# Expert weight preparation moved wholly into the attention steps, POOL's half of it tied to the accumulator's finish, in an MoE and attention block

## The chip, the cores and the metric

One core of one Trainium2 chip. The metric is the device time of one launch in microseconds (us), shown for the kernel before as the median of three runs. Engines are named as in the profile: PE (TensorE), DVE (VectorE), ACT (ScalarE), POOL (GpSimd), SP (SyncE, which here only issues DMAs).

## What is computed

Input q holds 8 x 512 tokens of 256 values. The output is q plus an attention of the normalized tokens against 1024 shared keys and values, plus a mixture of experts (one shared expert, eight routed ones, two chosen per token):

```python
xn = _layernorm(x)                                  # 4096 tokens x 256
scale = xn[:, ::step].reshape(b, -1)                # one factor per key, from 4 rows of each batch
qk = einsum('bsd,btd->bst', xn, k) * scale[:, None, :]
attn = einsum('bst,btv->bsv', softmax(qk), v)
shared = gelu(xn @ Wfc_s + bfc_s) @ Wproj_s + bproj_s
for e in range(8):                                  # gate: softmax over the two best experts
    h = gelu(xn @ Wfc[e] + bfc[e]) @ Wproj[e] + bproj[e]
    routed = routed + h * gate[:, e:e + 1]
return x + attn + (shared + routed)
```

All inputs are float32. The kernel multiplies in float16 with each operand split into a high half and a low residual, three products for each (high x high, high x low, low x high).

## The kernel before, in words

The kernel is one hand-ordered program. Each engine has its own list of instructions, written out in the order in which it runs, and the engines meet only at semaphores. Four stretches follow one another on PE:

- **Front steps** (i = 1 to 7, after a start-up for tile 0). Tokens come in 16 tiles of 256. A step computes the shared expert of tile i (`up_shared`, L1266; `down`, L1286), routes the tile (router L1238, `rank` L1249 to L1252), and transposes the next tile (`tr1`, L1202), which DVE copies to `x_t` (`copy_xt`, L794). DVE also makes the layer norm (`front_a`, `normalize` L844), the float16 split of it (`split_x_hi` L853, `split_x_lo` L858) and the slot numbers (`front_b`, its first instruction L874).
- **Attention steps** (u = 0 to 31, one for 128 queries). PE's list for a step is `transpose_probs(u)` L1352, `scores(u + 2)` L1338, `side_work(u)`, `values(u - 1)` L1406. `side_work` carries the routing of tiles 8 to 15: by u modulo 3, the router, the rank (L1249), or the transposition of a further tile. DVE's list is `finish(u - 2)` L991 (which adds the attention output to the accumulator `acc`), `p_lo(u)` L979 and L982, then in a step with u mod 3 = 0 the normalization L844, in the next one the split L853 and L858, then `scale_scores(u + 2)` L968, then the routing work (L808 to L836, or L874 to L888). ACT runs `p_hi(u)` L744, a piece of weight preparation, `exp(u + 2)` L735.
- **Routed steps**: 40 steps for blocks of tokens sorted by expert, in which SP loads the expert's packed weights from `wpack` (`load_fc`, `load_pj`, L462), the tokens (`load_slots`, L499) and the biases. The first block's tokens are transposed by PE already in attention step 29 (`tr2_first`, L1202), from the tile that SP loads first.
- **Last steps**: the shared expert for tiles 8 to 15, and POOL's gathers of routed results (L666), which DVE adds to `acc`.

The weight preparation is 16 jobs, one for each of the 8 experts' two matrices (1 MB each). SP loads a matrix to `w_stage` (`load_job`, L365), ACT scales it in place (`scale_w`, L676) and casts its high half to `w_split` (`split_w_hi`, L684), POOL subtracts (`split_w_lo`, L609: two halves of four 256-wide instructions each), and SP stores the 1 MB result to `wpack` (`store_job`, L375). Before, there are two buffers of each kind; four jobs run in the front steps (i = 1, 3, 5, 7) and twelve in attention steps 0 to 24. POOL also computes the reciprocal deviation of each tile (`inv_std`, L592), scatters the split tokens to `slots_x` (L619, four indirect DMAs for a tile), and adds the shared expert's output bias to each tile of `acc` (`add_bias`, L600), for which DVE's `evict_shared` and `finish` wait. The function names with their lines are all in the printed code:

```python
            for u in range(QT):
                k, phase = u // 3, u % 3
                i = NA + 1 + k
```

sets the phases named here; NA is 8, QT is 32, tile i is normalized, split and transposed in phases 0, 1 and 2.

## Time and profile before

| what | value |
|---|---|
| median of 3 runs | 867.32 us (866.02 to 872.22) |
| the profiled execution, its own time | 861.36 us |
| its span in the profile | 859.5 us |
| PE busy | 785.8 us, 91% of the span |
| DVE, ACT, POOL busy | 490.7, 441.0, 257.3 us |
| instructions | 20915 |

The span runs from the first to the last recorded instruction. 1.86 us of the execution's own time lie outside it. Windows are given in us from the span's start. The attention steps' matmuls run from 117.8 to 354.7 us of it, the routed steps from there to about 742 us. In the timelines a row is one instruction or a run of like ones; its first two numbers are start and duration, "x24" is the count, and the bracket at its end the idle time before it and what ended it.

### The profile page before, as it was taken

To read this page: it belongs to the slowest core of one execution; us is meant where nothing else is said; L and a number is where in the kernel's file an instruction comes from. 1 tells how busy PE (TensorE), PEld (TensorE's weight loads), DVE (VectorE), ACT (ScalarE), POOL (GpSimd) and SP (SyncE) were. 2 spreads that over 40 slices of the span, in tenths; PEclk is the share of its full clock that TensorE was granted. 3 is DMA by queue.
4 is the path that set the end of the run, shared out by engine and by line. 5 is a ranking of instruction groups with operands and counts; after the bars stand their busy time and mean duration, and the time that the engine had idled before them with its cause. 6 is when DMAs were issued, how large, how long until landed. Compare 5 with 4: busy or idle time off the path is not lost.

```text
span 859.5 us, 20915 instructions
## 1 busy us (share of the span) xinstructions
PE 785.8 (91%) x7222; PEld 661.5 (77%) x7222; DVE 490.7 (57%) x1144; ACT 441.0 (51%) x845; POOL 257.3 (30%) x318
## 2 busy tenths in 40 slices
PE   4888899699969899999999999999999999977893
PEld 3777776476647677999999989999999998865772
DVE  6888868888898776444434453333333333353464
ACT  6665466365636544565465555555555555524350
POOL 5666756557655730000000000000000000263655
PEclk9999999899979999999999999999999999996997
DMA  9464341647464535344322554454545452142334
GB/s 307 157 221 135 137 168 54 233 154 233 142 221 153 197 118 185 124 165 153 123 68 97 158 183 161 158 160 146 172 135 175 128 186 86 45 125 74 119 119 134
DMA packets 70379, 129.11 MB, mean 150 GB/s; under 512 B 12248, under 2 KB 56480, under 8 KB 63920
## 3 DMA queue, kind: packets, MB, share of 16 engines
q1 hardware_dynamic: 64176, 111.57, 39.3%
q0 software_dynamic: 6144, 16.79, 6.1%
q8 instruction: 33, 0.54, 0.2%
q14 instruction: 26, 0.21, 0.1%
HBM read 88.29 MB, written 40.04 MB: 149 GB/s over the span
## 4 chain that ended last, share of the span: by engine, by line
PE 69%; DVE 15%; issue 6%; POOL 4%; ACT 2%; DMA 2%; another core or an unknown queue 2%; DVEq 0%; SPq 0%; POOLq 0%; ACTq 0%
PE ps_h L1266 28%; PE ps_v L1286 27%; PE ps_v L1406 6%; PE ps_h L1338 4%; DVE xn L844 3%; PE ps_t L1202 2%; DVE prob L968 2%; POOL w_split L609 2%; PE ps_t L1352 1%; DVE p_t L982 1%; POOL y_rows L666 1%; DVE acc L1171 1%; DVE h_split L893 1%; ACT h L693 1%
## 5 line engine op out<-in xcount | busy, mean ns | idle before, releaser
L893 DVE TENSOR_TENSOR h_split<-h,h_split 128x512 f16<-128x512 f32 (+1 forms) x224 | 144.8, 655 | 164.0 <-ACT h_split L699 160.9
L693 ACT ACTIVATE h<-ps_h,b_fc 128x256 f32<-128x256 f32 (+1 forms) x320 | 125.9, 444 | 170.9 <-PE ps_h L1266 170.9
L666 POOL DMA_INDIRECT y_rows<-slots_y,y_row_all x64 | 64.4, 1007 | 480.9 <-DMA slots_y<-prob 437.8
L1266 PE MATMUL ps_h<-x_t,w_split 128*128 128x256 f16 (+1 forms) x1920 | 193.3, 261 | 0.0
L1286 PE MATMUL ps_v<-w_stage,h_split 128*128 128x256 f16 x1704 | 192.6, 273 | 0.0
L1266 PEld LDWEIGHTS ps_h<-x_t,w_split 128*128 128x128 f16 x1920 | 170.5, 98 | 17.0
L1286 PEld LDWEIGHTS ps_v<-w_stage,h_split 128*128 128x128 f16 x1704 | 165.1, 98 | 18.4
L699 ACT CAST h_split<-h 128x512 f16<-128x512 f32 (+1 forms) x224 | 131.1, 585 | 10.4 <-ACT h L693 0.4
L1266 PE MATMUL ps_h<-x_t,w_shared 128*128 128x256 f16 x768 | 94.0, 278 | 13.4 <-issue 13.0
L693 ACT ACTIVATE h<-ps_h,b_t 128x256 f32<-128x256 f32 x128 | 53.5, 468 | 99.6 <-PE ps_h L1266 58.1
L1266 PEld LDWEIGHTS ps_h<-x_t,w_shared 128*128 128x128 f16 x768 | 75.0, 99 | 29.4 <-issue 19.8
L1286 PE MATMUL ps_v<-w_shared,h_split 128*128 128x256 f16 x768 | 93.0, 280 | 3.5 <-issue 3.2
L1406 PE MATMUL ps_v<-v_split,p_t 128*128 128x256 f16 x768 | 93.0, 280 | 0.0
L1286 PEld LDWEIGHTS ps_v<-w_shared,h_split 128*128 128x128 f16 x768 | 76.6, 100 | 15.3 <-issue 4.5
L1338 PE MATMUL ps_h<-k_t,x_t 128*128 128x512 f16 x384 | 88.1, 379 | 0.0
L609 POOL TENSOR_TENSOR w_split<-w_stage,w_split 128x256 f16<-128x256 f32 x128 | 85.3, 699 | 4.0 <-ACT w_split L684 4.0
L619 POOL DMA_INDIRECT slots_x<-x_split,pos_i x64 | 65.0, 1016 | 69.4 <-DVE pos_i L888 53.2
L1406 PEld LDWEIGHTS ps_v<-v_split,p_t 128*128 128x128 f16 x768 | 75.5, 100 | 11.4
L1115 DVE SCALAR_TENSOR_TENSOR prob<-ps_v,b_pj 128x256 f32<-128x256 f32 x71 | 30.2, 425 | 87.0 <-PE ps_v L1286 87.0
L735 ACT ACTIVATE prob<-prob,neg_max 128x1024 f32<-128x1024 f32 x32 | 36.8, 1149 | 81.6 <-DVE neg_max L972 78.5
L1338 PEld LDWEIGHTS ps_h<-k_t,x_t 128*128 128x128 f16 x384 | 37.6, 98 | 38.1
L968 DVE CUSTOM_DVE_ANT_0 prob<-ps_h,scale_b 128x1024 f32<-128x1024 f32 x32 | 39.0, 1219 | 15.1 <-PE ps_h L1338 12.1
(153 smaller groups left out, 624.4 us busy)
## 6 DMA issues: line engine op xcount, KB each, us to landing
w_split<-wpack SPq DMA_DIRECT2D x17, 1024.0 KB, 5.1
w_stage<-wpack SPq DMA_DIRECT2D x17, 1024.0 KB, 5.0
wpack<-w_split SPq DMA_DIRECT2D x16, 1024.0 KB, 5.1
w_stage<-in_L_ffn_Wfc_dram SPq DMA_DIRECT2D x8, 1024.0 KB
w_stage<-in_L_ffn_Wproj_dram SPq DMA_DIRECT2D x8, 1024.0 KB
x_split<-slots_x SPq DMA_DIRECT2D x31, 256.0 KB, 3.5
slots_y<-prob SPq DMA_DIRECT2D x31, 256.0 KB, 3.2
b_pj<-in_L_ffn_bproj_dram SPq DMA_DIRECT2D x40, 128.0 KB, 3.1
```

Of the source, the lines that this page charges most:

```text
L609: ins = g.tensor_tensor(dst[:, 2048 + at:2304 + at], w_stage[par][:, at:at + 256], dst[:, at:at + 256], ALU.subtract)
L619: g.indirect_dma_start(slots_x, bass.IndirectOffsetOnAxis(ap=pos_i[par][:, c:c + 1], axis=0), x_split[i % 3][:, a, :], None).then_inc(s_sc ...
L666: g.indirect_dma_start(y_rows[:, n, kk, :], None, slots_y, bass.IndirectOffsetOnAxis(ap=y_row_all[:, c:c + 1], axis=0)).then_inc(s_gat[n], 16)
L693: ins = nc.scalar.activation(h32[:, hc, 0:n], ps_h[:, hc * TILE:hc * TILE + n], ACT.Gelu_apprx_tanh, bias=bias[:, hc:hc + 1], scale=1.0 / WS)
L699: nc.scalar.copy(h_split[par][:, 0, 2 * b:2 * b + 2, 0:n], h32[:, 2 * b:2 * b + 2, 0:n]).then_inc(s_hhi, 1)
L735: nc.scalar.activation(prob[par][:, :], prob[par][:, :], ACT.Exp, bias=neg_max[par][:, 0:1], accum_out=row_sum[par][:, 0:1]).then_inc(s_ex ...
L893: ve.tensor_tensor(h_split[par][:, 1, 2 * b:2 * b + 2, 0:n], h32[:, 2 * b:2 * b + 2, 0:n], h_split[par][:, 0, 2 * b:2 * b + 2, 0:n], ALU.s ...
L968: ve.tensor_tensor_reduce(out=prob[par][:, :], in0=ps_h[:, par * KEYS:(par + 1) * KEYS], in1=scale_b[b % 2][:, :], scale=1.0, scalar=-3.0e ...
L1266: ins = mm(ps_h[:, hc * TILE:hc * TILE + cols], wv[:, wl, c, hc * P:(hc + 1) * P], x[:, xl * DC + c, 0:cols], start=n == 0, stop=n == 3 * ...
L1286: ins = mm(ps_y[a][:, :], h_split[par][:, xl, c, a * P:(a + 1) * P], wv[:, wl, c, :], start=n == 0, stop=n == 3 * HC - 1)
L1338: ins = mm(ps_h[:, lo:lo + 512], x_t[:, i, ql * DC + c, par * P:(par + 1) * P], k_t[:, kl * DC + c, half * 512:(half + 1) * 512], start=n ...
L1406: ins = mm(ps_y[par][:, :], p_t[par][:, pl, c, :], v_split[:, vl, c, :], start=n == 0, stop=n == 3 * KC - 1)
```

## The change

The 16 jobs all run in the attention steps. There are four buffers for the loaded weights and four for the split ones: the two old pairs, and beside them `y_rows` and `h32` (loads), and the two `h_split` buffers (results), which the attention steps leave unused. Jobs 0 to 9 take two steps each (ACT scales at u = 2n and casts at 2n + 1, POOL subtracts one half in each of the two steps after that); jobs 10 to 15 have both of ACT's instructions in one step (u = 20, 21, 22, 24, 25, 26) and both of POOL's halves in one, two steps later (the last in step 28). A half is one 1024-wide instruction, no longer four of 256, and POOL waits before it for `finish(u - 2)`, DVE's first instruction of the step. In DVE's list `scale_scores` comes before the normalization and the split. `inv_std` runs at the start of the step in which the tile is normalized, no longer at the end of the one before. All 16 bias adds come after the last attention step, and only the last steps wait for them. The store of the last job is issued by SP after step 28, before it waits for all stores and loads the first routed weights.

```diff
+        stages = [t[:, :] for t in w_stage] + [y_rows[:, :, :, :].rearrange("p g k d -> p (g k d)"),
+                                               h32[:, :, :].rearrange("p c n -> p (c n)")]
+        splits = [t[:, :] for t in w_split] + [t[:, :, :, :].rearrange("p h c n -> p (h c n)") for t in h_split]
...
-        JOB_B = 2 + NA // 2
-        JOBS = 2 + 2 * EXPERTS
+        JOBS = 2 * EXPERTS
+        SLOW = 10
+
+        def scale_slot(n):
+
+            return 2 * n if n < SLOW else 2 * SLOW + (n - SLOW) + (n - SLOW) // 3
+
+        def hi_slot(n):
+            return 2 * n + 1 if n < SLOW else scale_slot(n)
+
+        def lo_slot(n, half):
+            return 2 * n + 2 + half if n < SLOW else scale_slot(n) + 2
...
-                if u % 2 == 0:
-                    m = JOB_B + u // 2
-                    if m <= JOBS:
-                        store_job(m - 1)
-                    if m + 1 < JOBS:
-                        load_job(m + 1)
+                if u == 0:
+                    load_job(3)
+                for n in range(JOBS):
+                    if u == lo_slot(n, 1) + 1:
+                        store_job(n)
+                        if n + 4 < JOBS:
+                            load_job(n + 4)
...
-                for at in range(piece * 1024, piece * 1024 + 1024, 256):
-                    ins = g.tensor_tensor(dst[:, 2048 + at:2304 + at], w_stage[par][:, at:at + 256], dst[:, at:at + 256],
-                                          ALU.subtract)
-                ins.then_inc(s_wlo, 1)
+                at = piece * 1024
+                g.tensor_tensor(dst[:, 2048 + at:3072 + at], src[:, at:at + 1024], dst[:, at:at + 1024],
+                                ALU.subtract).then_inc(s_wlo, 1)
...
-                add_bias(i)
-                if job_of(i) is not None:
-                    split_w_lo(job_of(i), 0)
-                    split_w_lo(job_of(i), 1)
...
+                if phase == 0 and i < SHARED:
+                    inv_std(i)
+                if u == 0:
+                    scatter(NA - 1)
+                for n in range(JOBS):
+                    for half in range(2):
+                        if u == lo_slot(n, half):
+
+                            wait_ge(pool, s_fin, u - 1)
+                            split_w_lo(n + 2, half)
+                if phase == 2 and i - 1 < SHARED:
+                    scatter(i - 1)
+
+
+            wait_ge(pool, s_bpj_in, 16)
+            wait_ge(pool, s_fin, QT)
+            for i in range(SHARED):
+                add_bias(i)
...
                 if u == 30:
                     act.wait_ge(s_bfc_in[0], 16)
+                    act.wait_ge(s_wlo, 2 * (JOBS + 1))
+                    act.wait_ge(s_w_out[2], 16 * (JOBS // 4))
                     gelu(R0, 0, b_fc[0], banks=(0, 1))
...
             def finish(u):
                 par = u % 2
-                dve.wait_ge(s_bias, u // SUB + 1)
...
                 p_lo(u)
+                if u + 2 < QT:
+                    scale_scores(u + 2)
                 if phase == 0 and i < SHARED:
                     front_b(norm=i)
                 if phase == 1 and i < SHARED:
                     front_b(split=i)
-                if u + 2 < QT:
-                    scale_scores(u + 2)
```

POOL's order in the first attention steps, before (L592 is the reciprocal deviation, L609 the halves of a job, L600 the bias add, L619 the scatter):

```order
L619 DMA slots_x<-x_split,pos_i 34048x512 x4
L592 TENSOR_TENSOR rstd<-var_eps,neg_half 128x2
L609 TENSOR_TENSOR w_split<-w_stage,w_split 128x256 x8
L600 TENSOR_TENSOR acc<-acc,b_pj_s 128x512
L609 TENSOR_TENSOR w_split<-w_stage,w_split 128x256 x8
L619 DMA slots_x<-x_split,pos_i 34048x512 x4
```

and the same place in the change (L602, L616 and L625 are those instructions):

```order
L602 TENSOR_TENSOR rstd<-var_eps,neg_half 128x2
L625 DMA slots_x<-x_split,pos_i 34048x512 x4
L616 TENSOR_TENSOR w_split<-w_stage,w_split 128x1024
L625 DMA slots_x<-x_split,pos_i 34048x512 x4
L602 TENSOR_TENSOR rstd<-var_eps,neg_half 128x2
L616 TENSOR_TENSOR w_split<-w_stage,w_split 128x1024 x3
L625 DMA slots_x<-x_split,pos_i 34048x512 x4
```

Where 17 of POOL's instructions (8 pieces, a bias add, 8 more pieces) stood in a row, single halves stand now, each behind a wait for DVE's finish.

DVE's order in attention step 0 of the next tile (L979 and L982 are `p_lo`, L844 the normalization, L968 and L972 `scale_scores`), before:

```order
L979 RECIPROCAL inv_sum<-row_sum 128x1
L982 TENSOR_TENSOR p_t<-ps_t,p_t 128x512 x2
L844 TENSOR_SCALAR xn<-acc,mean_var,rstd 128x256 x2
L968 ISA prob,row_max<-ps_h,scale_b 128x1024
L968 ISA row_max 128x1
L972 TENSOR_SCALAR neg_max<-row_max 128x1
```

and in the change:

```order
L988 RECIPROCAL inv_sum<-row_sum 128x1
L991 TENSOR_TENSOR p_t<-ps_t,p_t 128x512 x2
L977 ISA prob,row_max<-ps_h,scale_b 128x1024
L977 ISA row_max 128x1
L981 TENSOR_SCALAR neg_max<-row_max 128x1
L854 TENSOR_SCALAR xn<-acc,mean_var,rstd 128x256 x2
```

The normalization has moved behind the scaling of the scores.

## Rows read from the trace of the kernel before

**Rows 1.** Windows: length, busy us (x count) of PE, PEld, DVE, ACT, POOL, then clock, DMA.

```profile
38.00:117.80 79.80, 71.71 (x732) 63.33 (x729) 68.29 (x205) 48.52 (x82) 55.28 (x59) 0.98 0.46 156
117.80:354.70 236.90, 217.01 (x1679) 157.98 (x1678) 183.48 (x472) 124.18 (x167) 116.05 (x155) 0.96 0.48 163
354.70:742.00 387.30, 387.30 (x3894) 351.21 (x3892) 157.09 (x280) 206.03 (x480) 0.00 (x0) 1.00 0.44 143
```

**Rows 2.** Timeline of PE, attention steps 4, 27, 28 and 29.

```profile
162.73 0.19 PE L1249 MATMUL ps_v<-mask,before 128*128 128x8 f16 x1 [7.68 <-DVE acc L991]
...
162.89 4.59 PE L1406 MATMUL ps_v<-v_split,p_t 128*128 128x256 f16 x24
...
320.94 1.04 PE L1352 MATMUL ps_t<-ident_f,prob 128*128 128x128 f32 x8
...
327.02 1.04 PE L1352 MATMUL ps_t<-ident_f,prob 128*128 128x128 f32 x8
...
336.57 0.61 PE L1202 MATMUL ps_v<-ident_h,x_split 128*128 128x128 f16 x8
337.02 2.78 PE L1406 MATMUL ps_v<-v_split,p_t 128*128 128x256 f16 x24
```

**Rows 3.** Timeline of DVE, attention steps 3, 6, 27 and 28.

```profile
149.50 9.56 DVE L844 TENSOR_SCALAR xn<-acc,mean_var,rstd 128x256 f32<-128x256 f32 x2
...
176.60 1.16 DVE L844 TENSOR_SCALAR xn<-acc,mean_var,rstd 128x256 f32<-128x256 f32 x2
...
328.27 0.16 DVE L1014 TENSOR_SCALAR tab_x<-step_r 1x22 int32<-1x22 f32 x1 [0.19 <-issue]
328.41 0.48 DVE L991 SCALAR_TENSOR_TENSOR acc<-ps_v,inv_sum,acc 128x256 f32<-128x256 f32 x1
```

**Rows 4.** Timeline of POOL, start-up and attention steps 3 and 6.

```profile
10.49 2.12 POOL L625 TENSOR_TENSOR w_shared<-w_stage,w_shared 128x1024 f16<-128x1024 f32 x1 [4.48 <-ACT w_shared L710]
...
147.28 5.07 POOL L609 TENSOR_TENSOR w_split<-w_stage,w_split 128x256 f16<-128x256 f32 x8
...
153.54 5.05 POOL L609 TENSOR_TENSOR w_split<-w_stage,w_split 128x256 f16<-128x256 f32 x8
...
175.64 5.18 POOL L609 TENSOR_TENSOR w_split<-w_stage,w_split 128x256 f16<-128x256 f32 x8
```

**Rows 5.** Groups of DVE by shape, 117.8 to 354.7 us (busy, mean ns, idle before).

```profile
L982 DVE TENSOR_TENSOR p_t<-ps_t,p_t 128x512 f16<-128x512 f32 x64 | 40.9, 681 | 3.5 <-ACT p_t L744 3.5
L968 DVE CUSTOM_DVE_ANT_0 prob<-ps_h,scale_b 128x1024 f32<-128x1024 f32 x32 | 39.0, 1219 | 15.1 <-PE ps_h L1338 12.1 <-issue 2.9
L844 DVE TENSOR_SCALAR xn<-acc,mean_var,rstd 128x256 f32<-128x256 f32 x14 | 24.8, 1812 | 0.0
```

**Rows 6.** Groups of DVE by shape, 38 to 117.8 us.

```profile
L874 DVE TENSOR_TENSOR mask_sum<-mask_sum,mask 128x8 f16<-128x8 f16 x6 | 6.6, 1105 | 0.3 <-PE ps_t L1252 0.3
```

**Rows 7.** Waits, 38 to 117.8 us: total, times, longest.

```profile
PE ps_t L1202 <- DVE k_t L939: 4.1, 2, 2.2
PE ps_t L1238 <- DVE x_t L794: 4.0, 4, 1.7
```

**Rows 8.** Groups of ACT by shape, 117.8 to 354.7 us.

```profile
L735 ACT ACTIVATE prob<-prob,neg_max 128x1024 f32<-128x1024 f32 x32 | 36.8, 1149 | 81.6 <-DVE neg_max L972 78.5 <-issue 3.1
L744 ACT CAST p_t<-ps_t 128x512 f16<-128x512 f32 x64 | 34.2, 584 | 13.0 <-PE ps_t L1352 12.7
L676 ACT ACTIVATE w_stage<-w_stage 128x2048 f32<-128x2048 f32 x12 | 23.0, 1918 | 12.9 <-DMA w_stage<-in_L_ffn_Wproj_dram 12.9
```

**Rows 9.** Timeline of SP's queue, first loads for the routed steps.

```profile
329.26 0.37 SPq L462 DMA_DIRECT2D w_split<-wpack  x1
...
331.12 1.50 SPq L499 DMA_DIRECT2D x_split<-slots_x  x2
```

**Rows 10.** DMA issues: size of one, median us to landing.

```profile
wpack<-w_split SPq DMA_DIRECT2D x16, 1024.0 KB, 5.1
...
x_split<-slots_x SPq DMA_DIRECT2D x31, 256.0 KB, 3.5
```

More of the change, by code:

```diff
@@ L223, in moe_attention_block @@
         s_row_out = sem2("s_row_out")
-        s_w_in = sem2("s_w_in")
-        s_w_out = sem2("s_w_out")
+        s_wproj_in = sem("s_wproj_in")
+        s_w_in = [sem(f"s_w_in{n}") for n in range(4)]
+        s_w_out = [sem(f"s_w_out{n}") for n in range(4)]
         s_bt_out = sem("s_bt_out")
@@ L329, in rows @@
             return ap[ds(first, n), :].rearrange("(a p) d -> p a d", p=P)
-        def stored(m):
-            return 16 * ((m - 2) // 2)
-        def job_of(i):
-            return 2 + i // 2 if i % 2 == 1 and i < NA else None
-        JOB_B = 2 + NA // 2
-        JOBS = 2 + 2 * EXPERTS
+        JOBS = 2 * EXPERTS
[6 more added lines that the diff above has]
+            return 2 * n + 2 + half if n < SLOW else scale_slot(n) + 2
         block = ctx.enter_context(nc.Block())
@@ L374, in store_job @@
                     dst = wpack[(n - EXPERTS) * P:(n - EXPERTS + 1) * P, 4096:8192]
-                sp.dma_start(dst, w_split[m % 2][:, :]).then_inc(s_w_out[m % 2], 16)
+                sp.dma_start(dst, splits[n % 4]).then_inc(s_w_out[n % 4], 16)
             def store_row(i):
@@ L509, in store_slots @@
                 sp.dma_start(dst, src).then_inc(s_y_out[par], 16)
-            for par in range(2):
-                wait_ge(sp, s_w_out[par], 16 * EXPERTS)
+            for n in range(4):
+                wait_ge(sp, s_w_out[n], 16 * (JOBS // 4))
             wait_ge(sp, s_bt_out, 16)
@@ L673, in scale_w @@
             def scale_w(m):
-                par = m % 2
-                act.wait_ge(s_w_in[par], 16 * ((m + par) // 2))
-                nc.scalar.mul(w_stage[par][:, :], w_stage[par][:, :], WS).then_inc(s_wsc, 1)
+                src = w_stage[1][:, :] if m == 1 else stages[(m - 2) % 4]
+                if m == 1:
+                    act.wait_ge(s_wproj_in, 16)
+                else:
+                    act.wait_ge(s_w_in[(m - 2) % 4], 16 * ((m - 2) // 4 + 1))
+                nc.scalar.mul(src, src, WS).then_inc(s_wsc, 1)
             def split_w_hi(m):
-                par = m % 2
-                dst = w_shared[1] if m == 1 else w_split[par]
+                n = m - 2
+                src = w_stage[1][:, :] if m == 1 else stages[n % 4]
+                dst = w_shared[1][:, :] if m == 1 else splits[n % 4]
                 act.wait_ge(s_wsc, m)
-                if m >= 4:
-                    act.wait_ge(s_w_out[par], stored(m))
-                nc.scalar.copy(dst[:, 0:2048], w_stage[par][:, :]).then_inc(s_whi, 1)
+                if n in (2, 3):
+                    act.wait_ge(s_mm2, 2 * NA)
+                if n >= 4:
+                    act.wait_ge(s_w_out[n % 4], 16 * (n // 4))
+                nc.scalar.copy(dst[:, 0:2048], src).then_inc(s_whi, 1)
             def gelu(t, par, bias, first=False, n=TILE, banks=range(BANKS)):
@@ L716, in _ @@
                 gelu(i, i % 2, b_s)
-                if job_of(i) is not None:
-                    scale_w(job_of(i))
-                    split_w_hi(job_of(i))
                 if i == 2:
@@ L756, in _ @@
                     act.wait_ge(s_bfc_in[0], 16)
+                    act.wait_ge(s_wlo, 2 * (JOBS + 1))
+                    act.wait_ge(s_w_out[2], 16 * (JOBS // 4))
                     gelu(R0, 0, b_fc[0], banks=(0, 1))
-                m = JOB_B + u // 2
-                if m < JOBS:
-                    if u % 2 == 0:
-                        scale_w(m)
-                    else:
-                        split_w_hi(m)
+                for n in range(JOBS):
+                    if u == scale_slot(n):
+                        scale_w(n + 2)
+                    if u == hi_slot(n):
+                        split_w_hi(n + 2)
                 if u + 2 < QT:
```

57 lines of the change are left out of this document (23 added, 34 removed).

## The prediction

> **What bounds the kernel now.** I read the windows first. From 354.7 us PE is busy in every microsecond of the routed stretch, 387.30 of 387.30, and POOL does nothing there [rows 1]. Nothing in that stretch can get shorter by moving POOL's or ACT's work. What can change lies before it: the front steps leave PE idle for 79.80 - 71.71 = 8.1 us, the attention steps for 236.90 - 217.01 = 19.9 us [rows 1]. Then I asked the timelines what those 19.9 us are. They are not spread out. At attention step 4 PE stands for 7.68 us before its rank matmul and is released by DVE's finish, and the values matmuls behind it take 4.59 us, where the same 24 take 2.78 later [rows 2]. So a stall costs PE its length and 1.8 us more at a lower clock. The granted clock of the whole stretch, 0.96 against 1.00 in the routed steps, says the same [rows 1].
>
> DVE's timeline shows where it was: in step 3 the two normalizations took 9.56 us; in step 6 the same two took 1.16 [rows 3]. POOL ran 8 subtractions from 147.28 and 8 more from 153.54 to 158.59, and the normalization ended at 159.06 [rows 3, 4]. DVE did not compute for 9 us, it was shut out while POOL worked. Over the attention steps 14 normalizations have 24.8 us of busy time, a mean of 1812 ns [rows 5]. Two that are left alone take at most 1.16 us together [rows 3], which would make 8.1 us for 14, so at least 16.7 us went in this one line. Its neighbours, which read scores and probabilities from PSUM, are not touched: `p_lo` has a mean of 681 ns over 64 and the scaling 1219 ns over 32 [rows 5]. That difference is what the change rests on.
>
> The Trainium skill, "SBUF — State Buffer", section "Who interferes with whom", gives the mechanism: a VectorE copy, cast or tensor_scalar between SBUF operands can take the port pair that it shares with GpSimd, and whichever engine starts first keeps the pair until its instruction ends. The trace agrees on who is blocked, and not on how long: by that rule DVE would get in after one 256-wide piece, 5.07 / 8 = 0.63 us, while here it waited over all 17 pieces [rows 3, 4]. In step 6 it did get in early, 1.16 us beside a burst that ran from 175.64 to 180.82 [rows 3, 4]. By the rule taken strictly a 1024-wide piece blocks longer than a 256-wide one did (2.12 us against 0.63); that speaks against this part of the change and is rival 2.
>
> **The change, part by part.** The sum is made against the profiled execution.
>
> *Attention stalls.* POOL's half now starts when DVE has ended its first instruction of the step. A 1024-wide subtraction took 2.12 us at start-up, and four 256-wide ones in the attention steps 5.07 / 2 = 2.54 us [rows 4]. I take 2.12, the row of the same shape, and keep 2.54 as the other end. In that time DVE runs `p_lo` (2 x 0.68) and then the scaling (1.22): 2.58 us that read PSUM and are not blocked [rows 5], and in a step that PE bounds it waits for scores besides. The normalization comes behind both, so POOL has left by then in either case. In a step after a scatter POOL is late by some 2 us, but so is the normalization, behind PE's scores. What goes is PE's 19.9 us of idle time [rows 1] and two low-clock stretches of 1.8 us [rows 2]; I take all 23.5 us, and for the range 12 of it at the lower end. What is late next is PE itself: 6.08 us from one step to the next in steps 27 to 28 [rows 2].
>
> *Front steps.* POOL loses 8 pieces in each of four steps and a bias add in all seven, ACT 3.8 us in four steps. DVE's first routing instruction of a step, an addition of 128x8, has a mean of 1105 ns [rows 6]; 8 values in each partition are no work for 1105 ns where the scaling needs 1219 ns for 1024, so I read most of 6 x 1.1 = 6.6 us as blocked time; and the addition stands ahead of the x_t copy for which PE waits 4.0 us [rows 7]. This wait goes. PE's other wait, 4.1 us for the copied keys in two steps [rows 7], I let go by half, since in those steps DVE also carries the splits of keys and values. 8.1 - 2.1 = 6.0 us, and 1 us more for the same effect in the start-up step: 7 us, between 4 and 9.
>
> *ACT.* In the last six jobs both passes, 1.92 us each if the cast is as long as the scaling, come into one step beside an exponential and two casts: 3.84 + 1.15 + 1.17 = 6.2 us [rows 8] against PE's 6.08 [rows 2]. Three such steps in a row put ACT some 0.5 us behind. The exponential has waited 78.5 us for DVE in these 32 steps [rows 8], and it is made two steps ahead of its use. No cost; up to 3 us if semaphores add 0.5 a step.
>
> *The bias adds.* All 16 go to the routed steps, where POOL is idle for 387 us [rows 1], and are first wanted at 742 us. No cost. Behind them in POOL's list are only the gathers. The waits of DVE for them are gone.
>
> *The end of the attention steps.* This is where the change adds a wait. Before, the last job was stored at about step 24, and SP's wait for all stores was long over when DVE's tables were ready at 328.43; then the first weight load was issued at 329.26 and the token loads at 331.12 [rows 3, 9]. Now the last job's two halves wait for the finish of step 28, which ended at 328.89 [rows 3]. On that clock: 328.89 + 2 x 2.12 [rows 4] = 333.1; the store takes 5.1 us to land [rows 10] = 338.3 with 0.1 us for the issue; from there SP needs to the token load what it needed before, 331.12 - 328.43 = 2.69 us [rows 3, 9], and the tokens 3.5 us to land [rows 10] = 344.5. PE reached the transposition of these tokens at 336.57 and values(28) stands right behind it in PE's list [rows 2]. So PE stands still for 344.5 - 336.57 = 8 us in step 29, and if it ends like the other stalls it costs 1.8 us of low clock: 9.8 us. Bounds: 6 if the store lands quickly, 13 if POOL is a few us behind from the scatter of step 23 or needs 2.54 us a half. Two of the weights' loads come behind this too, but their users come later than the tokens' by more.
>
> *Sum.* 859.5 - 23.5 - 7 + 9.8 = 838.8 us of span; with the 1.9 us outside it 840.7. The median of the runs shown is 6.0 us above the profiled execution. If the length of DVE's shut-out is a matter of chance, as 9.56 against 1.16 suggests, part of those 6 us is that chance and goes too. I keep half: 843.7, forecast 844 us.
>
> **The rivals.**
>
> 1. *No stall in step 29* (POOL or the store is earlier than I think, or PE comes later). For it: in the 6.2 us steps of ACT, PE could slip by a little. Against it: the finish that opens the last half is at a fixed place of DVE's list. 844 - 9.8 = 834 us.
>
> 2. *The blocking only moves.* POOL comes out of the scatter late (four indirect DMAs in a step that also has a half), and the half behind it meets the normalization. One whole piece, 2.12 us [rows 4], is lost in each meeting. Seven tiles are normalized in these steps: 7 x 2.12 = 14.8 us, 859 us. Against it: the last seven normalization steps would all have to meet it, though DVE has 2.58 us of unblocked work first. The rule of the Trainium skill quoted above is this rival's, one instruction and no more.
>
> 3. *The long shut-outs are not POOL's bursts at all*, or come back in another line, and only the front's gain and the new stall are real: 844 + 23.5 = 867 us, no change. Against it is the match of the times, 158.59 and 159.06.
>
> 4. *Slower: the gate makes every half a collision.* If one of the instructions right behind the finish is in fact blocked by a 1024-wide POOL instruction, the gate aligns the two engines in every step. 20 steps carry one half, at 2.12 us each: 42 us, 886 us. It decides from the point where DVE's first blockable instruction comes within 2.12 us of the finish. Against it: the means of 681 and 1219 ns hold over steps both with and without POOL's work [rows 5]; they would have to hold only for short pieces.
>
> **How the numbers follow.** Forecast 0.55 (its own range 834 to 853), rival 1 0.13, rival 2 0.14, rival 3 0.11, rival 4 0.07. The range for 8 in 10 is 830 to 864: down to rival 1 with a few us more from the front, up past rival 2 but short of rival 3. A measurement of this kernel can tell about 1%, that is 858.6 and 876.0 us. Faster by over 1%: the forecast, rival 1 and half of rival 2, 0.75. Within 1%: the other half and rival 3, 0.18. Slower: rival 4, 0.07.
>
> **What would show it.** In the changed profile the normalizations' mean should be near 0.4 to 0.6 us and none above 2.5; PE's waits for DVE's finish in the rank should be under 2 us in all; the front stretch should be some 7 us shorter; the first routing addition should fall from 1.1 us to a few tenths; and the transposition of the first tokens in step 29 should stand for about 8 us, released by a DMA, with slow values matmuls behind it. If PE is idle in the middle of the attention steps by more than 5 us, the main step is wrong; if it isn't idle in step 29, the last one is.

## The result, and the profile after

The change makes the kernel faster: 845.55 us median (836.54 to 846.22, four runs) against 866.67 us (862.83 to 872.22, four runs of the kernel before). The ratio is 0.9728, with a 95% interval of 0.9656 to 0.98. The profiled execution took 836.54 us, its span is 834.7 us. The forecast of 844 us is met; what follows shows that two of its terms missed and, by luck, nearly cancelled.

I cut the span at the first scores matmul, at the first routed matmul behind the last attention step (two halves of the first block's up matmuls already run inside steps 30 and 31) and at the first matmul of the last steps. The change moved 10.3 us in the front, 13.9 in the attention steps and nothing after them:

| stretch | before | after |
|---|---|---|
| start-up and front steps | 117.8 us | 107.5 us |
| attention steps | 236.9 us | 223.0 us |
| routed steps | 377.3 us | 377.6 us |
| last steps | 127.5 us | 126.6 us |

The windows of the kernel after, with the columns of [rows 1]:

```profile
38.00:107.50 69.50, 66.90 (x703) 59.90 (x701) 55.65 (x188) 36.89 (x74) 28.47 (x29) 1.00 0.33 106
107.50:330.40 222.90, 214.12 (x1679) 157.57 (x1677) 158.10 (x471) 139.02 (x174) 108.06 (x75) 0.98 0.56 194
330.40:717.50 387.10, 387.02 (x3889) 350.68 (x3888) 166.06 (x280) 205.69 (x480) 23.78 (x16) 1.00 0.44 143
```

PE's idle time in the front steps fell from 8.1 us [rows 1] to 2.6, in the attention steps from 19.9 us [rows 1] to 8.8. POOL's 16 bias adds, 23.78 us, now lie under a PE that is busy for 387.02 of 387.10 us. DVE's busy time in the attention steps fell from 183.48 us [rows 1] to 158.10, though it does the same work there. The groups of DVE by shape in that stretch say which line lost most of these 25.4 us (busy, mean ns, idle before):

```profile
L991 DVE TENSOR_TENSOR p_t<-ps_t,p_t 128x512 f16<-128x512 f32 x64 | 41.5, 681 | 6.5 <-issue 3.6 <-ACT p_t L752 2.5
L977 DVE CUSTOM_DVE_ANT_0 prob<-ps_h,scale_b 128x1024 f32<-128x1024 f32 x32 | 39.2, 1224 | 20.2 <-PE ps_h L1347 20.2
L854 DVE TENSOR_SCALAR xn<-acc,mean_var,rstd 128x256 f32<-128x256 f32 x14 | 5.3, 420 | 0.0
L863 DVE CAST x_split<-xn 128x512 f16<-128x512 f32 x7 | 3.0, 426 | 0.5 <-issue 0.4
```

The 14 normalizations take 5.3 us where they took 24.8 [rows 5], 19.5 us less. The lines that read PSUM have kept their durations to within 5 ns, with POOL's 1024-wide halves beside them. The scaling, which waited 12.1 us for PE's scores [rows 5], waits 20.2: DVE is now ahead of PE. The small routing addition of the front steps has lost its blocked time too, 152 ns against 1105 [rows 6] (groups of DVE by shape, 20 to 107.46 us):

```profile
L884 DVE TENSOR_TENSOR mask_sum<-mask_sum,mask 128x8 f16<-128x8 f16 x8 | 1.2, 152 | 0.0
```

One step shows how the two engines pass each other. First DVE's timeline, then POOL's:

```profile
128.55 0.43 DVE L863 CAST x_split<-xn 128x512 f16<-128x512 f32 x1
...
130.82 0.49 DVE L999 SCALAR_TENSOR_TENSOR acc<-ps_v,inv_sum,acc 128x256 f32<-128x256 f32 x1
131.41 0.16 DVE L988 RECIPROCAL inv_sum<-row_sum 128x1 f32<-128x1 f32 x1
131.49 1.27 DVE L991 TENSOR_TENSOR p_t<-ps_t,p_t 128x512 f16<-128x512 f32 x2
132.70 1.23 DVE L977 CUSTOM_DVE_ANT_0 prob<-ps_h,scale_b 128x1024 f32<-128x1024 f32 x1
```

```profile
131.51 2.14 POOL L616 TENSOR_TENSOR w_split<-w_stage,w_split 128x1024 f16<-128x1024 f32 x1 [5.83 <-DVE acc L999]
133.80 0.99 POOL L625 DMA_INDIRECT slots_x<-x_split,pos_i  x1
```

POOL waited 5.83 us for the finish, worked from 131.51 to 133.65 while DVE read PSUM until 133.93, and was gone. In a step with a normalization the margin is thinner, since POOL's scatter and the reciprocal deviation stand ahead of the half. DVE, then POOL, in the next such step:

```profile
141.13 0.79 DVE L854 TENSOR_SCALAR xn<-acc,mean_var,rstd 128x256 f32<-128x256 f32 x2
```

```profile
139.31 2.12 POOL L616 TENSOR_TENSOR w_split<-w_stage,w_split 128x1024 f16<-128x1024 f32 x1
```

The half ends at 141.43, 0.3 us after the normalization has begun, and costs it less than 0.1 us (0.79 us for the pair against 0.73 in the quickest). The new wait stands where the forecast put it. PE's timeline in attention steps 28 to 30:

```profile
299.46 2.75 PE L1347 MATMUL ps_h<-k_t,x_t 128*128 128x512 f16 x12
310.16 1.03 PE L1211 MATMUL ps_v<-ident_h,x_split 128*128 128x128 f16 x8 [7.95 <-DMA x_split<-slots_x]
310.98 4.57 PE L1415 MATMUL ps_v<-v_split,p_t 128*128 128x256 f16 x24
```

PE stands for 7.95 us, and the values matmuls behind it take 4.57 us, where undisturbed ones take 2.78 [rows 2]. POOL's timeline and SP's queue show the chain that leads there:

```profile
294.73 4.22 POOL L616 TENSOR_TENSOR h_split<-h,h_split 128x1024 f16<-128x1024 f32 x2 [2.51 <-DVE acc L999]
```

```profile
292.29 7.08 SPq L384 DMA_DIRECT2D wpack<-h_split  x2
304.26 0.37 SPq L472 DMA_DIRECT2D w_split<-wpack  x1
...
306.11 1.51 SPq L509 DMA_DIRECT2D x_split<-slots_x  x2
```

The last two halves end at 298.95; some 5 us later, the time that such a store takes to land [rows 10], SP goes on to the routed loads (304.26) and the tokens (306.11), which PE gets at 310.16.

### The profile page after: what moved, and what is told of

The parts are those of the page before. It is cut to its first block, busy times and chain, and to the rows that moved or that the text cites. A ratio compares the mean times of both kernels' runs of the same rounds, so it can differ in the third digit from the quotient of the medians.

```text
span 834.7 us, 20811 instructions
## 1 busy us (share of the span) xinstructions
PE 780.4 (93%) x7222; PEld 659.7 (79%) x7222; DVE 462.7 (55%) x1144; ACT 441.4 (53%) x845; POOL 240.8 (29%) x216
## 4 chain that ended last, share of the span: by engine, by line
PE 82%; DVE 8%; issue 4%; another core or an unknown queue 2%; DMA 2%; POOL 2%; SPq 1%; ACT 0%; POOLq 0%; DVEq 0%
PE ps_h L1275 29%; PE ps_v L1295 28%; PE ps_v L1415 10%; PE ps_h L1347 9%; PE ps_t L1361 3%; PE ps_t L1211 2%; DVE h_split L903 2%; DVE acc L1179 1%; POOL y_rows L671 1%; DMA b_rows<-in_L_ffn_bfc_s_dram 1%; DVE xn L854 1%; DMA wpack<-h_split 1%; PE ps_v L1211 0%; DMA x_split<-slots_x 0%
## 5 line engine op out<-in xcount | busy, mean ns | idle before, releaser
L903 DVE TENSOR_TENSOR h_split<-h,h_split 128x512 f16<-128x512 f32 (+1 forms) x224 | 152.9, 692 | 160.4 <-ACT h_split L710 152.9
L710 ACT CAST h_split<-h 128x512 f16<-128x512 f32 (+1 forms) x224 | 130.8, 584 | 10.1
L1275 PE MATMUL ps_h<-x_t,w_shared 128*128 128x256 f16 x768 | 93.3, 278 | 14.3 <-issue 13.7
L1295 PE MATMUL ps_v<-w_shared,h_split 128*128 128x256 f16 x768 | 91.2, 275 | 9.1 <-issue 9.0
L1415 PE MATMUL ps_v<-v_split,p_t 128*128 128x256 f16 x768 | 90.8, 276 | 0.0
L625 POOL DMA_INDIRECT slots_x<-x_split,pos_i x64 | 64.1, 1002 | 17.5 <-issue 16.7
L977 DVE CUSTOM_DVE_ANT_0 prob<-ps_h,scale_b 128x1024 f32<-128x1024 f32 x32 | 39.2, 1224 | 20.2 <-PE ps_h L1347 20.2
L752 ACT CAST p_t<-ps_t 128x512 f16<-128x512 f32 x64 | 34.9, 585 | 26.0 <-PE ps_t L1361 25.5
```

What stands on the lines that cost most here:

```text
L625: g.indirect_dma_start(slots_x, bass.IndirectOffsetOnAxis(ap=pos_i[par][:, c:c + 1], axis=0), x_split[i % 3][:, a, :], None).then_inc(s_sc ...
L710: nc.scalar.copy(h_split[par][:, 0, 2 * b:2 * b + 2, 0:n], h32[:, 2 * b:2 * b + 2, 0:n]).then_inc(s_hhi, 1)
L752: nc.scalar.copy(p_t[par][:, 0, 4 * kk:4 * kk + 4, :], ps_t[:, kk * 512:(kk + 1) * 512].rearrange("p (c n) -> p c n", n=P)).then_inc(s_phi, 1)
L903: ve.tensor_tensor(h_split[par][:, 1, 2 * b:2 * b + 2, 0:n], h32[:, 2 * b:2 * b + 2, 0:n], h_split[par][:, 0, 2 * b:2 * b + 2, 0:n], ALU.s ...
L977: ve.tensor_tensor_reduce(out=prob[par][:, :], in0=ps_h[:, par * KEYS:(par + 1) * KEYS], in1=scale_b[b % 2][:, :], scale=1.0, scalar=-3.0e ...
L1275: ins = mm(ps_h[:, hc * TILE:hc * TILE + cols], wv[:, wl, c, hc * P:(hc + 1) * P], x[:, xl * DC + c, 0:cols], start=n == 0, stop=n == 3 * ...
```

## The experiments

By a shut-out I mean a DVE instruction that has begun and cannot proceed while POOL works; by the gate, POOL's wait for the finish ahead of each half. The theory: the time lay in DVE's shut-outs by runs of POOL instructions, and both the gate and the new order of DVE's list are needed to end them; what is left is the stall behind the last store. The rivals: the smaller number of instructions does it, or the order alone, or the gate alone, or the bias adds. The table has the stretches of each profiled execution (us), the median, and the ratio to the kernel before with its interval. Executions of the kernel before in these comparisons had medians of 864 to 869 us. A median of two runs can be off by several us, so I read the stretches first. They scatter too: four profiles with the front's code of the kernel before (the two in which only the order changed, the one with the gate alone, and its own) have fronts of 116.2 to 120.6 us, seven with the front's code of the change 106.9 to 108.9 us. Where the long shut-outs are gone and PE never stands at the end, the attention steps agree within 0.2 us (213.7, 213.7, 213.8).

| run | front | attention | last | median (runs) | ratio |
|---|---|---|---|---|---|
| 1024-wide pieces alone | 115.1 | 240.8 | 125.6 | 868.55 (6) | 0.9986 (0.9925 to 1.0047) |
| order alone | 120.6 | 233.4 | 128.8 | 863.35 (8) | 0.9987 (0.9953 to 1.0022) |
| bias adds alone | 114.7 | 225.8 | 134.8 | 856.71 (2) | 0.9859 (0.9758 to 0.996) |
| gate alone | 116.2 | 245.8 | 135.2 | 875.19 (2) | 1.0119 (1.002 to 1.0217) |
| change without gate | 107.1 | 228.2 | 133.3 | 848.22 (2) | 0.9761 (0.9676 to 0.9847) |
| change without order | 107.8 | 230.7 | 121.6 | 845.11 (2) | 0.972 (0.9628 to 0.9813) |
| change with 256-wide pieces | 107.7 | 224.7 | 132.7 | 839.66 (2) | 0.9658 (0.9578 to 0.9738) |
| jobs sooner | 108.9 | 213.7 | 134.5 | 834.02 (4) | 0.9588 (0.9565 to 0.961) |
| tokens first | 106.9 | 218.7 | 134.3 | 833.43 (2) | 0.9586 (0.9491 to 0.9681) |
| both of these | 107.3 | 213.7 | 135.1 | 833.27 (4) | 0.9621 (0.9543 to 0.9698) |
| jobs sooner, gathers cut | 107.7 | 213.8 | 96.4 | 797.89 (2) | 0.9225 (0.9136 to 0.9314) |

**1024-wide pieces alone**, on the kernel before.

```diff
-                for at in range(piece * 1024, piece * 1024 + 1024, 256):
-                    ins = g.tensor_tensor(dst[:, 2048 + at:2304 + at], w_stage[par][:, at:at + 256], dst[:, at:at + 256],
-                                          ALU.subtract)
-                ins.then_inc(s_wlo, 1)
+                at = piece * 1024
+                g.tensor_tensor(dst[:, 2048 + at:3072 + at], w_stage[par][:, at:at + 1024], dst[:, at:at + 1024],
+                                ALU.subtract).then_inc(s_wlo, 1)
```

> The kernel before with one edit: a half of a job is one 1024-wide POOL subtraction, not four of 256; nothing is gated and DVE's order is the old one. Theory A (DVE stays shut out as long as POOL's instructions follow one another without a pause): two halves, a bias add and two halves in a row still shut out the normalization for over 7 us in one or two places, its total in the attention steps stays at 15 to 25 us and PE stays idle there for 15 to 20 us. Theory B (the port is free at the end of each instruction, as the Trainium skill, SBUF, has it): no normalization takes longer than 2.2 + 0.4 us, its total falls below 15 us, PE's idle time there below 8 us. The time: A 858 to 870 us, B 845 to 855 us.

No change in the time (868.55 us, as theory A has it), and the clearest picture of the shut-out. PE idles 19.9 us in the attention steps, also as in A, but the normalizations take 34.5 us, more than the 15 to 25 expected, and the stretch is 3.9 us longer than before. DVE's timeline, then POOL's:

```profile
146.68 7.89 DVE L843 TENSOR_SCALAR xn<-acc,mean_var,rstd 128x256 f32<-128x256 f32 x2
154.50 1.21 DVE L967 CUSTOM_DVE_ANT_0 prob<-ps_h,scale_b 128x1024 f32<-128x1024 f32 x1
```

```profile
144.50 4.21 POOL L609 TENSOR_TENSOR w_split<-w_stage,w_split 128x1024 f16<-128x1024 f32 x2
148.68 1.26 POOL L600 TENSOR_TENSOR acc<-acc,b_pj_s 128x512 f32<-128x512 f32 x1
149.90 4.19 POOL L609 TENSOR_TENSOR w_split<-w_stage,w_split 128x1024 f16<-128x1024 f32 x2
```

POOL has five instructions in a row from 144.50 to 154.09. DVE's normalizations begin at 146.68 and end at 154.57: they sat behind four POOL instructions, past the boundaries at 148.7, 149.9 and 152.0, and got in when POOL stopped. The same happened at 193.40 (7.98 us) and at 238.70 (7.95 us), so three times, where one or two were expected. So a shut-out may last as long as POOL has instructions queued, whatever their width. This contradicts the Trainium skill, "SBUF — State Buffer", section "Who interferes with whom", by which the other engine gets the ports when the instruction that holds them ends; the measurement decides.

The other meetings here do go by that rule. Three more pairs here took 3.45, 3.07 and 3.38 us, each instruction of DVE getting in when one 1024-wide piece ended; beside 256-wide pieces the like pairs took 1.1 to 1.5 us. That is where the width counts, and why the total rose. A long queue does not decide it by itself either. At one step of the kernel before, the one that corresponds to 193.40 here, POOL had all 17 instructions in a row too, and each of DVE's two got in after one piece. DVE, then POOL:

```profile
196.19 1.51 DVE L844 TENSOR_SCALAR xn<-acc,mean_var,rstd 128x256 f32<-128x256 f32 x2
```

```profile
194.31 5.17 POOL L609 TENSOR_TENSOR w_split<-w_stage,w_split 128x256 f16<-128x256 f32 x8
199.44 1.28 POOL L600 TENSOR_TENSOR acc<-acc,b_pj_s 128x512 f32<-128x512 f32 x1
200.68 5.26 POOL L609 TENSOR_TENSOR w_split<-w_stage,w_split 128x256 f16<-128x256 f32 x8
```

What makes one meeting long and the other short no run tells.

**The order alone**, on the kernel before: `scale_scores(u + 2)` stands ahead of the normalization and the split. Two executions of it were profiled; the table has the second.

> The kernel before with DVE's order alone changed, once more for a profile of its own. As for b_swap: theory A, normalizations of over 5 us in one or two places, PE's idle time in the attention steps 12 to 20 us; rival, idle time under 6 us.

The ratio is 0.9987 over eight runs: POOL's 17 instructions outlast the 2.58 us that the order puts between them. One pair of normalizations still took 8.19 us, and PE idled 15.9 us, both as theory A has it. In the other profiled execution (872.25 us) two pairs were held off for so long (8.31 and 8.30 us), and the attention steps took 240.5 us. So the number of long shut-outs seems to differ between executions of one kernel.

**The bias adds alone**, on the kernel before: they move behind the attention loop, with DVE's waits for them.

```diff
-                if phase == 1 and i - 1 < SHARED:
-                    add_bias(i - 1)
...
+            wait_ge(pool, s_bpj_in, 16)
+            wait_ge(pool, s_fin, QT)
+            for i in range(SHARED):
+                add_bias(i)
```

> The kernel before with the bias adds alone moved behind the attention steps (and DVE's waits for them with them). Theory: the first routing addition in the front steps was blocked by the bias add behind the scatter: its mean there falls from 1105 ns to under 300, the front stretch up to the first scores gets 4 to 6 us shorter (117.8 to about 113), the rest of the 10 us that the changed kernel gained there is due to the jobs. Rival: the addition is blocked by the scatter's indirect DMAs or by the jobs: its mean stays above 700 ns and the front keeps within 1.5 us of 117.8. In the attention steps the bursts are one instruction shorter; the long shut-outs stay.

The front loses 3.1 us, a bit less than I expected, and DVE's first routing addition falls to 149 ns there, as in the full change. Of PE's two waits there, the one for the x_t copy fell from 4.0 us [rows 7] to 1.3, and the one for the keys stayed (6.0 us against 4.1); in the change they are 1.4 and 1.2. In the attention steps this execution had one long shut-out of the normalizations (8.51 us), the kernel before two (9.56 and 9.58), which one profile of each can't lay to the bias adds. So the bias adds are about a third of the front's 10.3 us, give or take the front's scatter. That the jobs which left it are the rest is a subtraction; no run moves them alone.

**The gate alone**, on the kernel before.

```diff
-                if u % 2 == 0 and JOB_B < JOB_B + u // 2 <= JOBS:
-                    split_w_lo(JOB_B + u // 2 - 1, 0)
-                    split_w_lo(JOB_B + u // 2 - 1, 1)
+                if JOB_B < JOB_B + u // 2 <= JOBS:
+                    wait_ge(pool, s_fin, u - 1)
+                    split_w_lo(JOB_B + u // 2 - 1, u % 2)
```

> The kernel before with the gate alone: in the attention steps each half of a job waits for the finish of its step, the second half in the next step; old job schedule (four in the front steps), two buffers, old DVE order, 256-wide pieces, bias adds in place. Theory A (the gate carries most of the attention steps' gain, the order the rest): no normalization over 4 us, but they stand close behind the finish and still meet a half, 10 to 20 us in all; and with two buffers ACT waits longer for the loads: the stretch falls from 236.9 to 222 to 230 us. Rival (the gate alone is enough): 214 to 218 us. Rival (two buffers are too few, ACT's wait for the weight load holds up exp): ACT waits over 25 us for DMA (12.9 before) and the stretch stays above 232 us.

Slower, by 1.2% (two runs, the interval 0.2 to 2.2%): theory A's stretch of 222 to 230 us missed, at 245.8, and the rival with too few buffers held. The normalizations did fall, to 11.5 us, though one still took 4.25, but a wait took their place. The waits from 100 to 370 us (total, times, longest):

```profile
ACT w_stage L676 <- DMA w_stage<-in_L_ffn_Wproj_dram: 43.2, 5, 11.3
...
PE ps_t L1352 <- DVE p_t L982: 17.3, 4, 5.8
ACT w_stage L676 <- DMA w_stage<-in_L_ffn_Wfc_dram: 15.0, 2, 12.0
```

ACT waits 58.2 us for weights, where it waited 12.9 [rows 8]. POOL gives a buffer back a step later, the load behind it starts later, ACT's probabilities stand in its list behind the late weights, and PE waits for them through DVE. With two buffers the gate costs more than it saves. In the change, with four, ACT does not wait for a weight load at all in the attention steps. The gate with four buffers and nothing else was not run.

**The change without its gate.**

```diff
-                            wait_ge(pool, s_fin, u - 1)
                             split_w_lo(n + 2, half)
```

> The changed kernel without POOL's wait for the finish ahead of each half; all else as changed. Theory A (the wait is what keeps POOL away from DVE's blockable instructions): POOL starts its halves as soon as ACT's cast is done, two in a row, at any place of DVE's step; normalizations and casts are shut out again, 5 to 15 us in all in the attention steps, PE idle there 3 to 12 us more than the changed kernel's 8.8. Rival (the wait does nothing; less work in a burst and DVE's new order are enough): PE's idle time stays at 8 to 10 us and the time within 3 us of the changed kernel's.

The normalizations come back to 16.9 us in all (mean 1249 ns), and PE idles 11.5 us, only 0.5 of it at the tokens, since the ungated halves are done sooner; 8.6 us are waits for DVE's finish. Three pairs of normalizations took 4.0 to 4.3 us, each of the two held off by one half, and none longer: with the new order and shorter runs of POOL's work the long shut-outs are already gone in this profile. Without the stall at the tokens the stretch is 227.7 us; the change's without its 9.8 us is 213.2. The gate is worth 14.5 us there, once its own stall is taken away; as the change stands, the gate also makes that stall, and is worth 5.2 us of the stretch (228.2 against 223.0). The medians, 848.22 and 845.55, don't tell the two kernels apart, which is what the rival had said of the time; its idle time of 8 to 10 us it missed. Theory A's own ranges were missed a little too: the normalizations lie above 15 us, and PE's idle time is up by 2.7 us and not by 3 or more.

**The change without its order**: the scaling behind the normalization and the split, as before.

> The changed kernel with DVE's old order (normalization and split ahead of the scaling), gate and jobs as changed. Theory (the gate needs the order: the normalization now comes 1.5 us behind the finish, and POOL's half lasts 2.13 us from there, in the steps after a scatter still longer): normalizations take 10 to 20 us in all in the attention steps instead of 5.3, none above 3 us, splits rise too, and the stretch gets 1 to 6 us longer than 223.0. Rival (the order does nothing, the gate is all): total under 7 us, stretch within 1 us of 223.0.

The attention steps take 7.7 us longer, which is more than I expected (0.4 us of it is a longer stall at the tokens, 8.37 against 7.95). The median of two does not show it, since this execution's last steps happened to be the shortest of all (121.6 us). The groups of DVE by shape:

```profile
L854 DVE TENSOR_SCALAR xn<-acc,mean_var,rstd 128x256 f32<-128x256 f32 x14 | 16.0, 1181 | 7.8 <-issue 5.6 <-POOL rstd L602 2.1
L863 DVE CAST x_split<-xn 128x512 f16<-128x512 f32 x7 | 7.8, 1108 | 0.0
```

Only `p_lo`, 1.27 us, now stands between the finish and these lines, and POOL's 2.13 us reach past it: both are blocked again. For the normalization there is a second tie: it needs the reciprocal deviation (L602), which POOL now computes in the same step with the half right behind it. In six steps the pair took 2.54 us, against 0.73 to 0.81 in the change.

**The change with 256-wide pieces**, four for each half, still gated.

> The changed kernel with a half as four 256-wide subtractions again, each group behind the gate. Theory (only when POOL works matters, not in how many pieces): normalizations stay at 5 to 6 us in all, the attention stretch within 1.5 us of 223.0; each half takes 2.5 us instead of 2.13, so the last store and with it the stall in step 29 is about 0.8 us later. Rival (the pieces matter: DVE gets in or is kept out by their number): normalizations change by more than 3 us in all or the stretch by more than 3 us.

The attention steps take 224.7 us, 1.7 more, and the stall at the tokens alone is 2.1 us longer (10.1 us instead of 7.95, where I expected 0.8). The normalizations take 8.3 us, not the 5 to 6 expected: a half lasts 2.54 us, so its last pieces meet them (pairs of 1.1 to 1.9 us against 0.75). PE shows no wait for that. Once gated, the width matters little.

**Jobs sooner**: on the change, the first double step is one job earlier, and the free step among them goes, so that the last halves run in step 26 instead of 28 and the last store is issued two steps earlier.

```diff
-        SLOW = 10
+        SLOW = 9
...
-            return 2 * n if n < SLOW else 2 * SLOW + (n - SLOW) + (n - SLOW) // 3
+            return 2 * n if n < SLOW else 2 * SLOW + (n - SLOW)
```

> The changed kernel with the jobs from 9 on at one a step without a gap (ACT at u = 18 to 24, the last halves in step 26, not 28). Theory: the last store is issued some 12 us earlier than before, the token load no longer waits for it, PE does not stand in step 29 (7.95 us there now, and 24 values matmuls at 4.57 us behind it): the attention stretch falls from 223.0 to 213 to 214 us and the median of the runs from 845.5 to 835 to 837 us. Rival (ACT at 6.2 us in seven steps running, or the loads of the last jobs, get late and hold up exp): PE's idle time moves into steps 19 to 26, the stretch stays above 218 us and the median above 841 us.

PE's timeline at the place where it stood for 7.95 us:

```profile
301.81 2.75 PE L1347 MATMUL ps_h<-k_t,x_t 128*128 128x512 f16 x12
304.47 0.62 PE L1211 MATMUL ps_v<-ident_h,x_split 128*128 128x128 f16 x8
304.93 2.78 PE L1415 MATMUL ps_v<-v_split,p_t 128*128 128x256 f16 x24
```

The stall is gone with its slow matmuls, the stretch is 9.3 us shorter, and PE is idle for 1.3 us of its 213.7. The last halves start at 287.00 instead of 294.73, 7.7 us sooner (9.2 counted from the first scores matmul) and not the 12 expected. At 834.02 us, just under the 835 to 837 expected, and a ratio of 0.9588 this version beats both kernels; its interval lies below the change's.

**Tokens first**: on the change, SP loads the tokens before it stores the last job and waits for the stores.

> The changed kernel with SP's order at the end alone changed: it loads the first two tiles of tokens ahead of the last store, the first weights after all stores as now. Theory (the stall in step 29 is the token load's queueing behind the last store): no wait of PE for x_split in step 29, but the first weights land at the same moment as before, about 310 us, so PE stands some 4 us in step 30, with slow matmuls behind: the attention stretch falls from 223.0 to 217 to 220 us. Rival (the tokens are late of themselves, by the scatters or the pads): the stall in step 29 stays above 5 us.

As in the theory, the tokens' stall goes and the stretch falls into 217 to 220 us; PE waits once, 2.95 us ahead of the first routed up matmuls, which then take 5.28 us instead of 2.78. The stretch is 4.3 us shorter than the change's. **Both edits together**, with the last store in its old place:

> The changed kernel with both mends: jobs from 9 on without a gap (last halves in step 26), and SP's token loads ahead of its wait for all stores; the last store stays in its place. Theory: with the jobs sooner PE has no stall left in steps 29 and 30 (1.3 us of idle time in the whole attention stretch), so the order of SP's loads has nothing left to give: attention stretch 213 to 214 us, median within 3 us of the 834 us of the version with the jobs sooner. Rival: the weights now come later behind the tokens and PE waits for them in step 30: stretch over 215 us.

213.7 us again: with the jobs sooner, nothing is left for SP's order to save.

**Jobs sooner, with the gathers cut** to the first round:

```diff
-                for kk in range(TOP):
+                for kk in range(TOP if u < GATHERS else 0):
```

> The version with the jobs sooner, without POOL's gathers of routed results in the last steps except the first 4 of 32 (8 of 64 indirect DMAs; DVE adds what lies in the buffers, so the routed part of the output is left out). It asks where the last stretch, 121.6 to 134.8 us in the ten profiles so far with one and the same code, gets its length and its scatter. Theory (PE's stops of about 1 us, for which the profile names no releaser, come from the gathers): they vanish after the first tile, PE's idle time in the last stretch falls from 34 us to 10 to 15, the stretch to 98 to 108 us. Rival (PE's instructions arrive late of themselves in this unrolled code): the stops stay, the stretch above 118 us.

This one is about the last steps, whose length goes from 121.6 to 135.2 us among all the other profiles, though PE's instructions there are the same in all. Windows of the last steps, first with all gathers (jobs sooner), then without:

```profile
700.20:834.70 134.50, 100.29 (x818) 81.05 (x815) 57.50 (x115) 44.52 (x96) 63.44 (x64) 0.87 0.34 99
```

```profile
699.09:795.50 96.41, 89.56 (x818) 79.73 (x815) 57.00 (x115) 44.23 (x96) 7.96 (x8) 0.99 0.19 61
```

PE has the same 818 matmuls. Beside 64 gathers it is idle for 34.2 us and runs at a mean clock of 0.87; beside 8 of them it is idle for 6.9 us at 0.99, both below what the theory gave (98 to 108 us, 10 to 15 idle). In the kernel after, PE's timeline shows what the idle time is:

```profile
743.77 0.82 PE L1275 MATMUL ps_h<-x_t,w_shared 128*128 128x256 f16 x6
744.75 0.60 PE L1275 MATMUL ps_h<-x_t,w_shared 128*128 128x256 f16 x4 [0.17 <-issue]
746.21 0.38 PE L1275 MATMUL ps_h<-x_t,w_shared 128*128 128x256 f16 x2 [0.85 <-issue]
747.65 0.38 PE L1275 MATMUL ps_h<-x_t,w_shared 128*128 128x256 f16 x2 [1.07 <-issue]
```

These are stops of about 1 us with no releaser (the longest in these steps is 1.8), in the middle of one tile's matmuls. They come with the gathers; what it is in a gather that stops PE (its traffic, its descriptors, or PE's own instruction supply beside them) no run here tells.

## Why the prediction was right, and where it was not

*Attention stalls: right.* The forecast took out 23.5 us and put in 9.8, net 13.7; the stretch lost 13.9. The gate keeps POOL clear of DVE's blockable lines (a half took 2.12 to 2.15 us, as taken), and the runs without gate and without order show that each is needed for the full gain. One reading was off: DVE's first normalization of the 9.56 us began at 149.50, inside the fourth of POOL's 17 instructions, so it waited over 14 of them and not over all 17. What the forecast did not see is the part of the buffers: it had no term for them, and the gate on two buffers made the kernel slower. The spreading of the jobs, which the four buffers allow, is the other part that it left out: without the gate no normalization waited for more than one half any more.

*The stall at the end: right.* 7.95 us and 1.8 us of slow matmuls against 8 and 1.8. From the start of POOL's last halves at 294.73 to the tokens' transposition at 310.16 it is 15.4 us, and the forecast's chain gave 344.5 - 328.89 = 15.6; SP was some 0.7 us quicker in it than taken, and the tokens 0.5 us slower. Taking it away gave 9.3 us back.

*The front: mis-sized.* The step that failed is "7 us, between 4 and 9"; it measured 10.3. I let PE's waits in the front go from 8.1 to 2.1 us, and they went to 2.6. The miss is in the rest, "1 us more". The window from 0 to 38 us answers: PE does 24.24 us of work in it, where before it did 21.78 (with the bias adds alone moved, 24.30). That is 2.5 us won in start-up in this pair of profiles. From 38 us on the idle time gives 5.5 us, and the remaining 2.3 go with the clock, 0.98 [rows 1] before and 1.00 now, a gain that I had counted in the attention steps and not here. The first and the last of these three are in part scatter. The three other profiles with the front's code of the kernel before did 22.6 to 24.4 us of work in the first 38 us, and from there on had clocks of 0.96, 0.96 and 1.00; the versions with the change's front did 23.8 to 24.7 us, with a clock of 1.00 in each. Of the three, only the idle time differs cleanly, 7.8 to 9.3 us against 2.4 to 2.6. So the front's gain is over the 7 us in the mean, 118.3 against 107.6 us, and how it splits beyond the 5.5 us is not settled.

*ACT and the bias adds: right.* ACT's scaling and cast were 1.92 and 1.90 us, the steps with both of them took 6.1 to 6.5 us on PE, no more than those with one, and PE shows no wait for ACT there. The adds cost the routed steps 0.3 us at most.

*From the profiled span to the median: the reasoning failed.* The sum was 838.8 us of span and it measured 834.7: 3.3 of the difference is the front, 0.9 the last steps. The step "I keep half" laid part of the 6.0 us between median and profiled execution to the chance of the shut-outs, and expected it to go with them. After the change the shut-outs are gone, and the median is 9.0 us above the profiled execution. Most of the scatter that the profiles show lies in the last steps, 121.6 to 135.2 us for the same work, and goes with the gathers' stops of PE, which this change leaves alone. So the front's 3.3 us too little and the scatter's 6.0 us too little (9.0 measured, 3 kept) were set against each other, and that 844 came out next to 845.55 is luck to that extent. The distance of the median from one execution is itself chance: the profiled one had last steps of 126.6 us, the third shortest among the thirteen profiles with all gathers.

*Rivals.* 1 (no stall) did not happen, until the jobs were moved. 2 (the blocking only moves) did not happen either; the change without its order is the case that it describes, at +7.7 us where it gave 14.8. Its ground, the shut-out of one instruction and no more, fits every meeting in that version and in the one without the gate, and is refuted as a general rule by the 7.89 us. 3 is refuted by the 24.8 us that became 5.3. 4 needed one of the PSUM readers to be blocked by a wide POOL instruction; their means stayed at 681 and 1224 ns.

## What to carry to other kernels

Look for a DVE instruction between SBUF operands whose mean is several times that of its quickest instances, and put POOL's timeline beside it: in the long shut-outs it counted how long POOL had work queued without a gap, in the short ones the width of one instruction. The cure here had four parts: spread POOL's work so that no long run of it stands in the queue, start each piece by a semaphore from a DVE instruction that reads PSUM, put at least a piece's length of PSUM-reading work behind it, and have enough buffers that the later POOL does not starve the loads. On this kernel the order alone gained nothing in the time and the gate alone lost 1.2%; taken out of the change, each cost 5 to 8 us of the attention steps. When work is moved towards the end of a stretch, follow its last store through every wait of the queue that issues the next stretch's loads; here two steps less on that chain were worth another 1.4% (845.55 to 834.02 us).

## What was not expected of the hardware

- POOL held DVE off across the boundaries of four consecutive instructions (7.89 us, and 7.98 us in another step), though in other steps of the same kernel the pair took 3.07 us and got in after one instruction for each of its two. Small operations are held off as well: an addition of 128x8 float16 had a mean of 1105 ns in the front steps and 149 once the bias adds behind the scatter had moved away.
- On POOL, one 1024-wide subtraction took 2.12 us, four 256-wide ones 2.54 us.
- Gathers issued by POOL go with stops of PE of about 1 us, 1.8 at the longest, that no semaphore explains: with 64 of them the last steps took 134.5 us, with 8 of them 96.4 us.
